# Attention on one core: the first pass 24 heads ahead instead of 22, the shift rows' chain a head later, and their DMAs as a step of their own

## The reference

```python
q = (x @ Wq.T + bq).reshape(B, N, HEADS, HEAD_DIM).transpose(0, 2, 1, 3)
k = (context @ Wk.T + bk).reshape(B, M, HEADS, HEAD_DIM).transpose(0, 2, 1, 3)
v = (context @ Wv.T + bv).reshape(B, M, HEADS, HEAD_DIM).transpose(0, 2, 1, 3)
attn = jax.nn.softmax(jnp.einsum('bhnd,bhmd->bhnm', q, k) * scale, axis=-1)
out = jnp.einsum('bhnm,bhmd->bhnd', attn, v)
out = out.transpose(0, 2, 1, 3).reshape(B, N, C) @ Wo.T + bo
```

## Time and profile before

| | |
|---|---|
| median of 3 runs | 1926.51 us (1926.38 to 1927.36) |
| the profiled execution | 1935.45 us, span 1933.5 us |
| attention, from `st 0` of turn 0 to the last `av` | about 865 to 1655 us |
| turns 1, 2, 5, 6 | 98.7 to 98.9 us each |
| turns 3 and 4 (the loop jumps back between them) | 102.1 and 103.6 us |
| mean granted TensorE clock | 0.971 of 2.4 GHz |

### The profile page before, as it was taken

The page is one execution under the profiler, slowest core; times in us unless marked ns, Lnnn a source line. Parts: engine busy times, 40 slices in busy tenths (PEclk is TensorE's granted clock), DMA queues, the critical chain, the costliest instruction groups (busy, mean ns, idle before and its releaser), DMA issues. The chain is left out here.

```text
span 1933.5 us, 38723 instructions
## 1 busy us (share of the span) xinstructions
PE 1824.7 (94%) x12524; PEld 1288.2 (67%) x12524; DVE 1430.8 (74%) x3030; ACT 1251.9 (65%) x3128; POOL 445.2 (23%) x629
## 2 busy tenths in 40 slices
PE   7899999999999999789999999989999999899988
PEld 5677777777777777564666666656666663588853
DVE  8988888888888888647686868667777775566348
ACT  5646464646464645348989898878888886266614
POOL 1312121212121212421222121222232222100006
PEclk9999999999999999898999999989999996799999
DMA  7122131313131313433334343334343423721266
GB/s 235 53 55 96 50 101 49 102 48 103 50 102 48 103 47 104 137 97 93 105 90 122 91 117 102 111 106 116 100 121 92 125 68 103 228 92 47 75 210 257
DMA packets 123884, 200.60 MB, mean 104 GB/s; under 512 B 27184, under 2 KB 48688, under 8 KB 123440
## 3 DMA queue, kind: packets, MB, share of 16 engines
q1 hardware_dynamic: 114480, 179.20, 30.1%
q0 software_dynamic: 9216, 18.89, 3.9%
HBM read 117.27 MB, written 29.88 MB: 76 GB/s over the span
## 5 line engine op out<-in xcount | busy, mean ns | idle before, releaser
L1961 ACT ACTIVATE a_shared<-a_shared,a_mx 128x512 f32<-128x512 f32 x512 | 344.4, 676 | 57.7 <-DVE a_mx L2024 57.5
L2024 DVE TENSOR_REDUCE a_mx<-a_shared 128x1 f32<-128x512 f32 x512 | 328.3, 682 | 37.9 <-PE a_shared L2171 36.2
L1954 ACT ACTIVATE a_probs<-a_scores 128x512 f32<-128x512 f32 x512 | 302.8, 607 | 58.8 <-PE a_scores L2182 58.6
L2171 PE MATMUL a_shared<-a_ks,a_qs 96*128 96x512 f32 x512 | 213.7, 438 | 13.8 <-ACT a_shared L1961 8.5
L2182 PE MATMUL a_scores<-a_qs,a_ks 98*128 98x512 f32 x512 | 211.3, 427 | 9.8 <-DMA a_qs<-a_shift_rows 5.2
L2143 PE MATMUL a_shared<-link 128*128 128x512 f32 x768 | 201.7, 399 | 9.7 <-DVE a_v L2018 7.4
L1086 PE MATMUL m_proj<-m_xt_hi,link 128*128 128x512 f32 x448 | 182.2, 407 | 3.9 <-DVE m_acc L780 3.5
L2171 PEld LDWEIGHTS a_shared<-a_ks,a_qs 96*128 96x128 f32 x512 | 96.2, 194 | 132.9 <-ACT a_shared L1961 59.5
L600 ACT ACTIVATE m_xw<-m_added,m_wdt 128x64 f32<-128x64 f32 x256 | 55.8, 329 | 192.7 <-DVE m_xdt L868 192.7
L2143 PEld LDWEIGHTS a_shared<-link 128*128 128x128 f32 x768 | 146.6, 192 | 47.3 <-DVE a_v L2018 10.9
L1087 PE MATMUL m_proj<-m_xt_lo,link 128*128 128x512 f32 x448 | 176.5, 394 | 0.0
(11 more groups left out here) (305 smaller groups left out, 3828.2 us busy)
## 6 DMA issues: line engine op xcount, KB each, us to landing
m_dec<-step_decay SPq DMA_DIRECT2D x64, 256.0 KB, 4.1
a_qs<-link SPq DMA_DIRECT2D x256, 64.0 KB, 2.0
m_ce<-run_decay SPq DMA_DIRECT2D x128, 112.0 KB, 3.1
a_ks<-a_k_hi POOLq DMA_DIRECT2D x192, 64.0 KB, 2.4
e_x<-x SPq DMA_DIRECT2D x11, 1024.0 KB, 5.6
m_xt_in<-x_t_in SPq DMA_DIRECT2D x8, 1024.0 KB, 9.6
m_x_tok<-x_in SPq DMA_DIRECT2D x8, 1024.0 KB, 5.4
x<-m_x_tok SPq DMA_DIRECT2D x32, 256.0 KB, 2.8
```

The costliest lines, as they stand in the source:

```text
L1954: act.activation(probs[:, n % 2, h, :], scores[t.score_bank(n, h)][:, :], ACT.Exp, scale=-1.0).then_inc(exp_ready, 1)
L1961: act.activation(scored[:, :], scored[:, :], ACT.Exp, scale=-1.0, bias=mx[:, i % 2, j, h:h + 1], accum_out=den[:, i, j, h:h + 1]).then_inc ...
L2024: dve.tensor_reduce(mx[:, i % 2, j, h:h + 1], bank(what)[:, :], AX.X, ALU.min).then_inc(mx_ready, 1)
L2171: pe.matmul(bank(what)[:, :], qs[0:STACK, t.slot(i), h, j * P:(j + 1) * P], ks[0:STACK, t.slot(i), h, :], start=True, stop=True).then_inc( ...
```

## The change

The first pass runs 24 heads ahead. The chain of a group is placed one `st` head later after the group's last `p1` head (which itself comes two heads earlier), and `range` no longer follows the last total at once. SP's wait and its four DMAs for the shift rows leave the step `split` and get a step `rows` of their own, one head behind `split`. `parts_of`, which places `fetch`, is not touched.

```diff
-FIRST_MAXIMUM = 22
+FIRST_MAXIMUM = 24
 MAXIMA = [5, 5, 3, 4, 4, 3, 3, 1, 8, 3, 5, 4, 4, 3, 5, 4]
...
-RANGE_LAG, LOG_LAG, SPLIT_LAG = 1, 2, 3
+RANGE_LAG, LOG_LAG, SPLIT_LAG, ROWS_LAG = 2, 3, 4, 5
...
             ending.extend([[lag, what, group, d] for lag, what in
-                           ((RANGE_LAG, "range"), (LOG_LAG, "log"), (SPLIT_LAG, "split"))])
+                           ((RANGE_LAG, "range"), (LOG_LAG, "log"), (SPLIT_LAG, "split"), (ROWS_LAG, "rows"))])
...
         for entry in list(ending):
             entry[0] -= 1
-            if entry[1] == "range":
+            if entry[0] == 0 and entry[1] == "range":
                 totals(0)
...
-                elif kind == "split":
+                elif kind == "rows":
                     sp.wait_ge(rows_ready, t.at(KT, i + 1))
                     rows = qs[STACK:STACK + 2, t.slot(i)].rearrange("p h (j b n) -> p (h j) b n", j=TT, n=AD)
                     for b in range(P // AD):
```

## The result

After the change the kernel takes 1957.59 us (median of 4 runs, 1955.58 to 1959.60), before 1926.55 (4 runs, 1926.38 to 1927.36): ratio 1.016, 95% interval 1.0143 to 1.0178, or 31 us slower. The forecast was 1952.0 and "slower". One execution of a kernel further down took 2572.7 us, at a mean granted clock of 0.65, and counts in no ratio.

What follows compares the result with a forecast made beforehand. TensorE's own stream was taken to set the pace (96.56 of a 98.7 us turn). Terms 1.8 - 10.2 + 9.8 + 11.1 + 3.5 + 9.5 = +25.5 us on 1926.51 gave a median of 1952.0 us; range 1936 to 1972.

Steps and rivals of the forecast that it cites:

- the old three: Waits predicted to vanish: `L2143` on `a_v`, VectorE in `range`, and `a_scores` on shift rows in group 2.
- the waits that go: TensorE's waits for `a_v` and group 2's shift rows vanish as the chain comes earlier: -10.2 us.
- the last turn: Fetch slips ahead of the last four rows DMAs on SP, making `st 48` late: +9.5 us.
- Start: First sequence's `st 0` waits for two more first-pass heads and their totals: +1.8 us.
- Stack of group 2: New TensorE wait at `p1 32` for the stack's DMAs, in all turns but turn 4: +9.8 us.
- Stack of group 0': New TensorE wait at `p1 0'` for the next sequence's stack, seven times 1.4 to 1.7 us: +11.1 us.
- The clock: One more fall of TensorE's clock to 1.2 GHz than before, after the new waits: +3.5 us.
- Clock falls at most new waits: Rival: five to ten more clock falls than before instead of one, 1966 to 1984 us; chance 0.15.
- Half hidden: Rival: the two stacks cost 10 us together and the rows land at once, 1935 us; chance 0.13.
- Faster: Rival: VectorE's 41.9 us of waiting are the real brake and stacks land before needed, 1917 us; chance 0.06.
- Nothing: Rival: waits that go and come are equal, rows late by less than the other engines, 1926 us; chance 0.04.

Runs made afterwards that it cites:

- a kernel further down: Kernel before with the rows in a step of their own behind `split`, so the fetch goes first; first of two measurements: 1941.2 us, ratio 1.0074.
- The best kernel: Changed kernel with fetch behind the rows, 23 ahead, stack DMAs shared 12 and 12, MAXIMA 5, 4, 4 (`p1 32` in front of `st 8`): 1910.27 us, ratio 0.9897.
- the second profile: The changed kernel measured again, unchanged, on the chip of two other kernels: 1957.84 us, ratio 1.0159 to the kernel before.

## Why the prediction was right, and where its terms were off

The predicted signs all came: two waits for `a_qs` a turn, the old three gone, the fetch ahead of the rows, the long wait ahead of `st 48`. The signed sum was 25.5 us and the medians differ by 31.0. How the 31 split depends on the side from which the fetch is taken. Put back in the changed kernel it is worth 19 us (forecast 9.5), and all else is 11.6 (forecast 16.0; ratio 1.006). Put ahead in the kernel before it is worth 13 to 14, which leaves 17 to 18 for all else. The terms below err both ways, the waits that go by some 6 us, the last turn by 4 to 9.5, so that the total came within 5.5 us is in part luck.

**Start, +1.8.** `st 0` of turn 0 starts at 868.2, in six profiles with 24 ahead at 867.3 to 869.7 (mean 868.3), in three with 22 and the old chain at 865.2 to 867.6 (mean 866.4): +1.9. Right, though each set spreads over 2.4 us.

**The waits that go, -10.2.** They went, but this term was too small by some 6 us. Turn 6 of the changed kernel takes 99.85 us and stands 3.6 of them for the two stacks: 96.3 without. The best kernel's turn of 96.4, with no stack wait, says the same. Before: 98.8. So 2.4 us a turn go where the listed waits gave 1.45 (8.7 in six turns). The rest goes with the chain's place, which I had priced at nothing beyond TensorE's own rows. The run with the chain one head earlier shows that it counts by itself: 9 us back, with VectorE standing 32.5 us in `range`. How it acts is shown in part: the 2.1 us at `p1 48` are VectorE's standing. The longer stand at the loop's jump and the longer low clock of that profile are only seen beside it, and no experiment separates VectorE's standing from the place.

**Stack of group 2, +9.8.** 1.54 to 1.86 us in an undisturbed turn, 3.07 in turn 1 and none in turn 4, 12.1 in all eight, 11.0 without turn 0. The refill starts 0.09 us after `st 63`, the 0.95 us sooner that the term had taken off. Right to 2.3 us, and turn 4 without it was forecast. Every kernel with `p1 32` ahead of V has this wait; in the last one it is gone.

**Stack of group 0', +11.1.** Seven waits of 1.57 to 2.08 us, 13.1 in all. Right to 2.0 us, and shown: 23 ahead takes these away, and 16 us with them, although it stands 2.3 us longer at `p1 32`. The some 5.6 us beyond the change in standing fit the clock, low for 6.8 us in its turns 1 to 6 instead of 23.9.

**The clock, +3.5.** In turns 1 to 6 the clock was low for 10.2 us before, 23.9 in this profile, 17.1 in the second one of the same kernel. Turns 5 and 6 of this profile stand equally long (3.6 us) and differ by one fall of 3.4 us: 101.3 and 99.9, so a low microsecond costs 0.4 us; over turns 1 to 6 of twelve of the profiles (all that are used but that with 22 and the late chain) a fit of their length, less all of TensorE's listed standing, to their low time gives 0.4 too. That is +3 to +6. The size was right; "one more fall" was not: there are several short ones. At the loop's jump TensorE stands 4.3 us at `st 1` and 1.5 at `p1 24`, before 2.5 and 2.3: 1.0 us more, which no term had. Turns 3 and 4 together take 206.2 us, before 205.7.

**The last turn, +9.5.** The step that failed most, in size. The mechanism is as written but for the ring order. The rows were transposed by 1641.62, and stood 12.2 us for their issue behind the fetch, from 1653.87 on. Then the last `e_w1s`, issued at 1653.00, landed at 1658.31 and `st 48` began at 1658.44, 2.53 us behind the last issue of the rows. In five kernels whose `st 48` waits for the rows with no load ahead of them that is 1.87 us, so what lay ahead in the rings cost 0.7 us here, 0.2 in the second profile and 1.1 in the kernel before with the fetch ahead. "The rows cannot pass the `e_w1s` data" was too strong: in the second profile `st 48` began at 1656.01, and the last `e_w1s` landed at 1656.37. The Trainium skill (DMA: Bandwidth & Descriptors, "Queues, rings and completion order") has each DMA engine consume its ring in order, but says that completion is not first in, first out for what one engine issues. The second profile agrees with the latter. The term's 5.4 us behind the last `e_w1s` issue gave nearly the same time (1658.4) as 2.0 us behind the rows' own last issue (1657.9), so the experiment does not need the rule.

Three things were missing. The fetch took SP 26.4 us (1627.42 to 1653.83), not 24.8. The baseline was wrong: I measured from `st 48` at 1634.85, in an execution whose clock had been low since 1611.4. In the kernel before with the even fill, `st 48` comes 70.2 us after the turn's start, in the profile of before 72.3. And the change had just made that baseline earlier, as `st 32` no longer waits 2.4 us for the rows of group 2 in the last turn: the kernel with the fetch behind the rows takes 22.2 us from `st 31` to `st 48` against 28.0. A late transfer costs its distance to when it would be wanted in the new kernel, not in the old. Last, after 13.5 us of standing the clock was at 0.54 up to `st 63`: 4.7 us more than with the fetch behind the rows, for which the term had no place (the profile of before, with its low clock, takes as long there, 15.8 us).

**What is left.** As measured the terms but the last add up to 15 to 18 us with the loop's jump, and the 2.4 us at `st 32` of the last turn come off; the ratio of 1.006 says 11.6. One to four microseconds are not accounted for.

**The rivals.** Clock falls at most new waits: no; in turns 1 to 6 there are five low stretches of 3.4 to 6.8 us for eleven waits, against one of 10.2 us before. That is four more, not far from the five of this rival, but each is short: 13.7 low us in all cost some 5.5 us, not 14. Half hidden: no, the stacks were late in full. Faster: its gain is real (2.4 us a turn in all, whether by VectorE's standing or by the chain's place), its condition, that the stacks come in time, did not hold; where it does, in the last kernel, 20 us are won. Nothing: no.

One part I did not see: with 24 ahead and the old lags the rows must leave `split`, or the kernel is a deadlock, as 24 ahead and nothing else is. The step of its own is enough to make 24 possible, since the kernel with the chain one head earlier has it with the old lags. By the list the longer lags alone would do too, as they put `split 1` behind `stack 2`; that was not run.

Open: why 24 ahead with an even fill won 15 us when its waits shrank by 6, how the earlier chain's 9 us come about, and what VectorE's standing in `range` costs the kernel before beyond the listed waits for `a_v`.

## What to carry to other kernels

When a look-ahead is lengthened, price it at each resource that the leading pass takes over from the trailing one: one step here moved a wait of 1.7 us in or out, and what separates two places in the order is the work between them (a matmul of 0.235 us or a projection), not a count of steps. When a step of one queue is split in two, look for everything that was placed relative to the old step; here the loads of the next stage slipped in front of four transfers of 4 KB and cost 13 to 19 of the 31 us. A wait that ends within 0.1 us of another is listed under the later one only: compare how long the same matmul stands, not the rows of waits. Take a late transfer's baseline from the kernel without the lateness, and at its own clock.

## What the runs showed of the hardware

TensorE's granted clock was at 0.50, which is 1.2 GHz, in stretches of 3.4 to 51.2 us, and a low microsecond cost some 0.4 us, not the whole microsecond. Standing was no sufficient cause: turn 6 of the changed kernel stood for 1.6 and 2.0 us at 1.00. In the 13.5 us of standing ahead of `st 48` it fell, at 1648.9, when TensorE had done nothing since 1644.9. The profile of before was 8.9 us above its median, and its 51.2 us at 1.2 GHz lay just where the change's largest term was measured.

Sixteen loads of 256 KB took SP 20.4 us to issue, 1.27 each, against 0.6 to 0.7 for the 64 KB ones of the stacks, before and after alike, and for the 4 KB ones of the rows. The rows stood 12.2 us behind the issuing and, from their last issue on, 2.5 us in flight instead of 1.9.
